# Attention: GpSimd sums the rotated halves and makes q's low half, ScalarE normalises the input

## The reference, cut to what matters

```python
def _layernorm(x, axis=-1, eps=1e-05):
    m = jnp.mean(x, axis=axis, keepdims=True)
    v = jnp.var(x, axis=axis, keepdims=True)
    return (x - m) / jnp.sqrt(v + eps)
...
    def _apply_rope(x, cos, sin):                    # attention 0 alone
        x_r, x_i = (x[..., ::2], x[..., 1::2])
        out_r = x_r * cos - x_i * sin
        out_i = x_r * sin + x_i * cos
...
    attn = jnp.einsum('bhqd,bhkd->bhqk', q, k) * SCALE     # causal, softmax
    out = jnp.einsum('bhqk,bhkd->bhqd', attn, v)
    return out @ wo.T
...
h = h + _L0_attn_ref(_layernorm(h, axis=-1), ...)    # 32 heads of 16, 8 of k and v
h = h + _L1_attn_ref(_layernorm(h, axis=-1), ...)    # 16 heads of 32, 4 of k and v
```

## Time and profile before

| | us |
|---|---|
| median of 3 runs (lowest, highest) | 2572.29 (2571.46, 2572.30) |
| the profiled execution, its span | 2573.25, 2571.2 |
| busy in the span: TensorE | 2268.0 (88%) |
| VectorE | 1787.5 (70%) |
| ScalarE | 1394.1 (54%) |
| GpSimd | 859.1 (33%) |

### The profile page before, as it was taken

How to read it: one execution, slowest core, us unless ns; L and a number is a source line. 1 busy time by engine, 2 the same in 40 slices (tenths; PEclk the granted TensorE clock), 3 DMA queues, 4 the chain that set the end, 5 groups by cost and what they waited for, 6 DMA issues and landing times. The chain is left out here.

```text
span 2571.2 us, 43226 instructions
## 1 busy us (share of the span) xinstructions
PE 2268.0 (88%) x13188; PEld 1134.2 (44%) x13188; DVE 1787.5 (70%) x3114; ACT 1394.1 (54%) x2214; POOL 859.1 (33%) x869
## 2 busy tenths in 40 slices
PE   7999999948888885389999995999996899999997
PEld 2333333315666663134444442666662344444443
DVE  6666666637999885675444673777765888788873
ACT  4666666634555554475222661555553666666663
POOL 2222222214444441042000360333322554455552
PEclk9999999979999997699999997999997999999999
DMA  4555555433322211122111223222221011111101
GB/s 117 133 132 131 131 131 130 115 98 137 106 61 61 61 54 34 42 77 73 58 49 53 88 77 102 71 82 73 78 62 42 28 43 50 38 41 49 42 25 49
DMA packets 144173, 194.53 MB, mean 76 GB/s; under 512 B 32549, under 2 KB 76165, under 8 KB 144058
## 3 DMA queue, kind: packets, MB, share of 16 engines
q1 hardware_dynamic: 117434, 159.58, 20.7%
q10 hardware_dynamic: 26624, 33.56, 4.8%
HBM read 125.17 MB, written 42.21 MB: 65 GB/s over the span
## 5 line engine op out<-in xcount | busy, mean ns | idle before, releaser
L330 DVE TENSOR_REDUCE tm_negmax<-tm_s 128x1 f32<-128x512 f32 x512 | 323.4, 678 | 168.5 <-PE tm_s L374 168.3
L291 ACT ACTIVATE tm_prob<-tm_s 128x1024 f32<-128x1024 f32 x256 | 257.6, 1023 | 142.2 <-PE tm_s L394 137.8
L1978 PE MATMUL f_part<-f_xhi,gu 128*128 128x512 f16 x704 | 270.0, 384 | 14.7 <-ACT f_firstg L1799 4.3
L1978 PE MATMUL f_part<-f_xlo,gu 128*128 128x512 f16 x704 | 269.2, 382 | 0.0
L411 PE MATMUL tm_o<-tm_prob,tm_vt 128*64 128x512 f32 x1024 | 255.4, 620 | 0.0
L2000 PE MATMUL f_pz<-dn,f_ghi 128*128 128x512 f16 x704 | 216.2, 382 | 27.3 <-ACT f_zc L1831 27.3
L1768 POOL TENSOR_TENSOR f_firstg<-f_firstg,f_secondg 128x512 f32<-128x512 f32 x88 | 148.5, 1688 | 198.8 <-DVE f_secondg L1874 198.8
L374 PE MATMUL tm_s<-tm_qk 96*128 96x512 f16 x512 | 199.6, 392 | 14.9 <-DMA tm_qk<-tm_xs 14.4
L394 PE MATMUL tm_s<-tm_qk 98*128 98x512 f16 x512 | 194.7, 383 | 0.8 <-DMA tm_qk<-tm_mrow 0.8
L248 POOL TENSOR_TENSOR tm_hn<-tm_nd,tm_rows 128x1024 f32<-128x1024 f32 x32 | 75.2, 2349 | 311.6 <-DMA tm_rows<-rden 311.6
L948 PE MATMUL a_bankB<-a_wqkv,a_xhi 128*128 128x512 f16 x512 | 158.0, 391 | 3.9 <-DVE a_xlo L786 3.9
(11 more groups left out here) (188 smaller groups left out, 5617.5 us busy)
## 6 DMA issues: line engine op xcount, KB each, us to landing
tm_qk<-tm_xs SPq DMA_DIRECT2D x384, 64.0 KB, 2.1
tm_xqk<-in_qk ACTq DMA_DIRECT2D x32, 512.0 KB, 4.5
a_hin<-h SPq DMA_DIRECT2D x64, 256.0 KB, 2.7
a_hres<-h SPq DMA_DIRECT2D x64, 256.0 KB, 2.8
h<-a_hout SPq DMA_DIRECT2D x64, 256.0 KB, 2.0
f_hin<-h SPq DMA_DIRECT2D x64, 256.0 KB, 2.7
f_hres<-h SPq DMA_DIRECT2D x64, 256.0 KB, 2.8
tm_vt<-in_vt ACTq DMA_DIRECT2D x32, 256.0 KB, 3.0
```

The lines of the kernel that those rows point to most:

```text
L291: nc.scalar.activation(prob[b][:, 2 * h:2 * h + 2, :], s2[:, i % 2, :, :], ACT.Exp, scale=SCALE).then_inc(exp_done, 1)
L330: nc.vector.tensor_reduce(negmax[u][:, m:m + 1], s1[:, p % BANKS, :], AX.X, ALU.max, negate=True).then_inc(s1_read, 1)
L1978: last = nc.tensor.matmul(part[q % BANKS][:, :], (gate, up)[which][:, j, m * P:(m + 1) * P], xparts[x][u][:, j, :], start=x == 0, stop=x == 1)
```

## The change

Three pieces of work change engines. The sum `rot` goes from VectorE to GpSimd and is cut in two, q's columns behind `crossed` of q, k's behind `crossed` of k. q's low half goes from VectorE to GpSimd, at the end of its step, in both stages; k's stays on VectorE. `xn` goes from VectorE to ScalarE, at the end of its step, in both stages, as one activation that scales by `rstd` and adds `shift_by` = -mean x rstd, which VectorE makes (`offset`). The waits follow; ScalarE's high half of q now waits for q's part of the sum only. The new functions of GpSimd, `rotate` and `q_lo`, and ScalarE's `x_normalised` stand in full in the diff.

```diff
@@ gpsimd
                 if inside(t, TILES) and rope:
                     wait_alone(pool, s["pool_passed"], s[("q_copied", "kv_copied")[part]], t + 1)
-                    if part == 0:
-                        wait_alone(pool, s["pool_passed"], s["rot_done"], t)
+                    wait_alone(pool, s["pool_passed"], s["rot_done"], 2 * (t - 1) + part + 1)
...
+            def rotate(t, part):
+
+                if inside(t, TILES) and rope:
+                    cols = (slice(0, DQ), slice(DQ, DQ + DKV))[part]
+                    wait_alone(pool, s["pool_passed"], s["turned_done"], 2 * t + part + 1)
+                    wait_alone(pool, s["pool_passed"], s["crossed_done"], 4 * t + 2 * part + 2)
+                    if part == 0:
+                        wait_alone(pool, s["pool_passed"], s["qhi_done"], t)
+                        wait_alone(pool, s["pool_passed"], s["qlo_done"], t)
+                    else:
+                        wait_alone(pool, s["pool_passed"], s["khi_done"], t)
+                        wait_alone(pool, s["pool_passed"], s["klo_done"], t)
+                    pool.tensor_tensor(rot[:, cols], turned[:, cols], crossed[:, cols], ALU.add)\
+                        .then_inc(s["rot_done"], 1)
+
+            def q_lo(t, u):
+
+                if inside(t, TILES):
+                    wait_alone(pool, s["pool_passed"], s["qhi_done"], t + 1)
+                    src = rot if rope else qkv[u]
+                    pool.tensor_tensor(qs[:, :, :, 1, :], src[:, 0:DQ].rearrange("p (h r d) -> p r h d", h=HKV, r=R),
+                                       qs[:, :, :, 0, :], ALU.subtract).then_inc(s["qlo_done"], 1)
...
                 cross(n + 2, u, 0)
+                rotate(n + 2, 0)
                 cross(n + 2, u, 1)
+                rotate(n + 2, 1)
+                q_lo(n + 2, u)
@@ scalar, copy_q
+                    wait(act, s["qlo_done"], t - 1)
@@ scalar, qk_hi
-                        wait(act, s["rot_done"], t + 1)
+                        wait(act, s["rot_done"], 2 * t + 1)
...
+                    if rope:
+                        wait(act, s["rot_done"], 2 * t + 2)
                     nc.scalar.copy(kp[:, 0, :, :, :], src[:, DQ:DQ + DKV].rearrange("p (h d) -> p h d", h=HKV)
...
+            def x_normalised(t, u):
+
+                if inside(t, TILES):
+                    wait(act, s["offset_done"], t + 1)
+                    wait(act, s["xT_ready"], t - 1)
+                    nc.scalar.activation(xn[u][:, :], hin[u][:, :], ACT.Identity, scale=rstd[u][:, :],
+                                         bias=shift_by[u][:, :]).then_inc(s["xn_done"], 1)
...
                 x_hi(n + 3, 1 - u)
+                x_normalised(n + 4, u)
@@ vector
-            def x_normalised(t, u):
+            def offset(t, u):
+
                 if inside(t, TILES):
                     wait(dve, s["rstd_done"], t + 1)
-                    wait(dve, s["xT_ready"], t - 1)
-                    nc.vector.tensor_scalar(xn[u][:, :], hin[u][:, :], mv[u][:, 0:1], rstd[u][:, :],
-                                            ALU.subtract, ALU.mult).then_inc(s["xn_done"], 1)
+                    nc.vector.tensor_scalar(shift_by[u][:, :], mv[u][:, 0:1], rstd[u][:, :], -1.0,
+                                            ALU.mult, ALU.mult).then_inc(s["offset_done"], 1)
...
                 turn(n + 2, u, 0)
-                x_normalised(n + 4, u)
                 y_lo(n - 1)
                 turn(n + 2, u, 1)
-                rotate(n + 2)
+                offset(n + 4, u)
                 probs_lo(n)
-                qk_lo(n + 2, u)
+                k_lo(n + 2, u)
                 x_lo(n + 3, 1 - u)
```

More of the change, by code:

```diff
@@ L468, in attention @@
         stats, mv, rstd = pair("stats", [P, 6], F32), pair("mv", [P, 2], F32), pair("rstd", [P, 1], F32)
-        veps = pair("veps", [P, 1], F32)
+        veps, shift_by = pair("veps", [P, 1], F32), pair("shift_by", [P, 1], F32)
         xn = pair("xn", [P, DM], F32)
@@ L503, in attention @@
         stored = [sem(f"stored{i}") for i in range(2)]
-        names = ("stats_done mv_done veps_done rstd_done xn_done xT_ready xhi_done xlo_done q_ready kv_ready "
+        names = ("stats_done mv_done veps_done rstd_done offset_done xn_done xT_ready xhi_done xlo_done q_ready kv_ready "
                  "q_copied kv_copied turned_done crossed_done rot_done qhi_done qlo_done khi_done klo_done "
@@ L798, in turn @@
                     wait(dve, s[("q_copied", "kv_copied")[part]], t + 1)
+                    wait(dve, s["rot_done"], 2 * (t - 1) + part + 1)
                     cols = (slice(0, DQ), slice(DQ, DQ + DKV))[part]
@@ L804, in turn @@
                         .then_inc(s["turned_done"], 1)
[L806 to L812, removed]
             def inverse_sums(t):
@@ L837, in y_lo, with k_lo @@
                         .then_inc(s["yTlo_done"], 1)
-            def qk_lo(t, u):
+            def k_lo(t, u):
                 if inside(t, TILES):
-                    wait(dve, s["qhi_done"], t + 1)
                     src = rot if rope else qkv[u]
-                    nc.vector.tensor_tensor(qs[:, :, :, 1, :], src[:, 0:DQ].rearrange("p (h r d) -> p r h d", h=HKV, r=R),
-                                            qs[:, :, :, 0, :], ALU.subtract).then_inc(s["qlo_done"], 1)
                     wait(dve, s["khi_done"], t + 1)
```

## The result

| | before | after |
|---|---|---|
| median of 6 runs (lowest, highest), us | 2572.30 (2570.09, 2573.04) | 2580.44 (2574.65, 2583.07) |
| ratio after / before, 95% interval | | 1.0030 [1.0017, 1.0043] |
| span of the profiled execution, us | 2571.2 | 2575.6 |

The account below looks back on a forecast made before the run. Attention 0 was taken to be bound by a ring of waits through in-order engines, attention 1 by TensorE. +18 us in attention 0 and -2 in attention 1 gave +16, 2588 us against the median; range 2569 to 2603.

Parts of the forecast that it names:

- The ring in attention 0: Attention 0, chain through VectorE, GpSimd and ScalarE from `mx` to next `mx`: 13.37 us a tile, against 12.77 before.
- The waits ahead of the sums: GpSimd, attention 0: waiting for its own `crossed` costs 0.18 us before each sum, plus 0.10 for q's three further waits.
- 27 periods: Attention 0: 27 tile periods, each 0.60 us longer, add 16.2 us.
- fill and drain: Attention 0's first and last tiles: +1.5 us for four fill tiles, +0.5 for two drain tiles.
- The lock: Attention 0: VectorE's `kp` blocks against GpSimd's q low half, so `xlo` starts at 12.14 us, not 11.77.
- No lock: Rival, attention 0: `kp` goes first or the two don't exclude each other; period 13.00, total 2578 us; 17 in 100.
- Attention 1: TensorE's waits for `yTlo` shrink since `xn` no longer precedes it: -2 us, bounds 0 and 3.7.
- `xn` on ScalarE: Last in ScalarE's step, 0.58 us, covered by half a period before TensorE wants it; uncovered, 0.6 us on top.
- The faster rivals: Attention 0: GpSimd's sum is cheap, 2564 us, 12 in 100; or TensorE's 11.46 us a tile binds, 2535, 3 in 100.

Follow-up runs that it names:

- experiment 4: Changed kernel with GpSimd's wait for its own `crossed` put last ahead of each sum and two implied waits left out: 2569.84 us, 0.9995 of the kernel before.
- experiment 6: Changed kernel, but in attention 0 q's low half stays on VectorE, ahead of k's: 2582.57 us, 1.0042 of the kernel before.
- experiment 1: Kernel before with the whole change in attention 1 alone, attention 0 as before: 2562.71 us, ratio 0.9962.
- experiment 5: Kernel before with two VectorE instructions swapped in both stages, `yTlo` ahead of `xn`, no work changing engines: 2560.46 us, ratio 0.9951.
- experiment 9: Kernel before with `xn` on ScalarE in both stages, `shift_by` behind `pTlo`, and GpSimd's `rstd` behind all of `crossed`: 2532.22 us, ratio 0.9843.
- experiments 3 to 9: From the kernel before with only `xn` moved to ScalarE (2559.08 us) to that with `rstd` behind all `crossed` and `shift_by` behind `pTlo` (2532.22 us).

## Why the prediction was right in sign and wrong in size

- **The ring in attention 0: right.** 13.37 us a tile was forecast, 13.48 measured in the loop; `crossed` 6.51 us behind `mx` (6.42), the sum of q 8.35 (8.25), its 1.27 us (1.26), q's low half 1.15 (1.15), `xlo` 12.32 (12.14).
- **The waits ahead of the sums: too small.** 0.28 and 0.18 us were forecast, 0.37 each measured, and no more than 0.18 needed (experiment 4). "I take 0.10" for the waits beside the own one was half of their 0.19 for q's sum, and for k's sum I had left them out.
- **27 periods: too many at the full price.** In the loop it was 13.475 - 12.75 = 0.72 a tile on the mean, in the steps written out, which have no increments behind the waits, 0.18. 22 x 0.72 + 5 x 0.18 = +17 where the forecast had +16.2; with fill and drain the traces show +15.8 and +19.6 for +18. The term stands by two errors that cancel, and that is luck.
- **The lock: right.** `kp` at 0.92 us and `qs` and the sum in experiment 6 are further rows for it; they end 0.28 and 0.32 us behind the instruction that they met. By the Trainium skill, page "SBUF — State Buffer", section "SBUF: two separate sides", the later of the two blocks for the whole of the other's instruction; the trace agrees in both directions. *No lock* is out. The prediction left the same meeting out of what it took as given: `rstd` beside `turned` of q, 0.96 us where 0.55 is its length without it. That was so before the change as well; in the changed kernel it is 0.97 to 1.06 us, which is why `crossed` starts 0.09 us later than forecast.
- **Attention 1: the step that failed.** "I take -2; the bounds are 0 and 280 - 276.27 = 3.7, all of TensorE's idle time." It was -10.8 in the profile, -9.4 in experiment 1 (-10.0 in its trace) and reached by `yTlo` alone in experiment 5. With -10 in its place the forecast's own sum gives +8, as measured. The bound came from busy time, and the busy time of matmuls covers pauses: 0.28 to 0.38 us a tile in the loop, where the waits had 0.2 in 11 tiles and nothing in the others. Summed over the 29 tiles of the stage whose two groups could be read, the starts came 8.0 us nearer to each other; the 1 or 2 us beside them have no cause shown. The 3.7 us were also those of a stretch of 280 us, and the stage is 370 long. The place and the mechanism, TensorE's wait for `yTlo` behind `xn`, were in the prediction; the size was read from the wrong column. The Trainium skill, page "Trainium Kernel Development and Optimization", section "Performance Expectations", calls matmul busy time a bad metric because matmuls are pipelined; the trace agrees, with 276.27 of 280 us busy over those pauses, and I had not applied it.
- **`xn` on ScalarE: hidden, as forecast**, at 0.81 us instead of 0.58: in both stages no tile of the loop waits for it on TensorE.
- **The faster rivals.** The 11.46 us that TensorE's busy time gives for attention 0 were out of reach of this change, but an order comes near them: experiment 9 has 11.66 us. What the ring hung on was not the load on VectorE but that GpSimd took `rstd`, which is wanted late, ahead of `crossed`, which is wanted first.
- **What stays open.** The two stages run alone add up to +3 and together give +8; the intervals allow it, and in the traces the two give +18.7 and -10.0, which is +9. Fill and drain move an execution by some us, but no run separates that from an effect of one stage on the other.

## What to carry to other kernels

Where engines run in order and wait for one another, follow the ring from one tile's instruction to the same one of the next before counting loads: 1.1 us of work a tile taken off the busiest engine made the stage slower, and moving `rstd` back in the list of a half-idle engine, with `shift_by` put behind `pTlo` (experiments 3 to 9), gave 27 us. Judge TensorE's slack by the spacing of starts between groups of matmuls, not by its idle column. In a loop where each wait brings a counter's increment, put the wait that comes last at the end and drop what another implies; in the steps without increments the same order brought nothing.

## What the runs showed of the hardware that I had not expected

- In GpSimd's loop two more waits with their increments behind the late one cost 0.19 us; with one of them ahead of it and one left out nothing of that shows (0.37 against 0.18 us). In the steps written out it is 0.13 against 0.17.
- A ScalarE activation that scales and shifts each row by a value of its own takes 0.81 to 0.82 us for 128x512 f32, where a copy of the same shape takes 0.58.
- With two SBUF inputs on VectorE and a GpSimd instruction it is the later that waits, on either engine: `kp` 0.42 to 0.92, in attention 1 to 1.28; GpSimd's sum 0.45 to 0.76; `turned` 0.69 to 1.20 us. `rstd`, of a single column, takes 0.92 to 0.96 us behind the start of `turned` and 0.55 alone. The other way round nothing shows: in experiment 9 `rot` starts 0.07 us behind `rstd` and takes its 0.83 us all the same.
